# First row maxima of the second layer taken in the last expert steps of a two-layer transformer kernel

## The reference, cut to what matters

```
x = x + attention0(layernorm(x))     # causal, 16 heads of 8, with bias
x = x + experts0(layernorm(x))       # 8 experts, the best 2 of each row, 128 -> 512 -> 128, exact GELU
x = x + attention1(layernorm(x))     # no mask, 16 heads of 8
x = x + fp4_mlp(layernorm(x))        # gate, up, down (352 wide), each block of 16 rounded to FP4
```

## Time and profile before

| | |
|---|---|
| median of three runs | 2203.91 us |
| the profiled execution, its own time | 2203.53 us |
| its span in the profile | 2201.8 us |
| busy: TensorE, VectorE, ScalarE, GpSimd | 1959.7, 1631.8, 1428.1, 1127.5 us |
| expert stage, first and last expert matmul | 838.3 to 1109.6 us |
| layer_one, first matmul | 1113.27 us |

### The profile page before, as it was taken

How to read it: one execution, slowest core, us unless ns; L and a number is a source line. 1 busy time by engine, 2 the same in 40 slices (tenths; PEclk the granted TensorE clock), 3 DMA queues, 4 the chain that set the end, 5 groups by cost and what they waited for, 6 DMA issues and landing times. The chain is left out here.

```text
span 2201.8 us, 48376 instructions
## 1 busy us (share of the span) xinstructions
PE 1959.7 (89%) x13892; PEld 998.6 (45%) x14051; DVE 1631.8 (74%) x4372; ACT 1428.1 (65%) x3354; POOL 1127.5 (51%) x1882
## 2 busy tenths in 40 slices
PE   5999999999999957999969888899988889898985
PEld 1455555555555537999922223333333333333333
DVE  7888888887888734443367788888888887888855
ACT  0666766666676644555537777777777777777774
POOL 6334746546474263344345465656665665664221
PEclk7999999999999978999979999999999999999998
DMA  3342323222232122222322212122222212211100
GB/s 97 86 137 73 95 78 94 83 83 86 83 91 81 42 81 71 71 75 84 95 67 66 64 59 66 58 64 63 63 63 66 65 56 63 65 57 54 57 6 15
DMA packets 144100, 155.34 MB, mean 71 GB/s; under 512 B 32160, under 2 KB 111712, under 8 KB 143584
## 3 DMA queue, kind: packets, MB, share of 16 engines
q1 hardware_dynamic: 131888, 131.84, 20.0%
q0 software_dynamic: 8192, 16.79, 2.7%
q10 hardware_dynamic: 3760, 3.62, 0.6%
HBM read 102.87 MB, written 47.71 MB: 68 GB/s over the span
## 5 line engine op out<-in xcount | busy, mean ns | idle before, releaser
L2370 DVE TENSOR_REDUCE l_rowmax<-pair 128x2 f32<-128x1024 f32 x512 | 597.1, 1217 | 134.1 <-PE pair L2046 134.1
L2245 ACT ACTIVATE l_probs<-bank 128x512 f32<-128x512 f32 x1024 | 554.9, 602 | 86.1 <-PE bank L2057 60.7
L1008 DVE CUSTOM_DVE_ANT_0 pair<-pair,mask_rows_q 128x512 f32<-128x512 f32 (+3 forms) x1024 | 476.7, 519 | 80.0 <-PE pair L718 72.9
L887 ACT ACTIVATE l_probs<-bank 128x256 f32<-128x256 f32 (+3 forms) x769 | 307.9, 444 | 106.9 <-PE bank L732 102.7
L718 PE MATMUL pair<-k_stack,q_stack 96*128 96x512 bf16 (+3 forms) x1024 | 316.0, 313 | 22.0 <-DVE l_rowmax L1008 13.5
L2057 PE MATMUL bank<-q_stack,k_stack 128*128 128x512 bf16 x929 | 298.5, 387 | 28.8 <-ACT l_probs L2245 13.6
L2069 PE MATMUL bank<-l_probs,v_aug 128*32 128x512 f32 x2048 | 278.3, 615 | 4.4 <-ACT l_oT L2302 2.6
L2046 PE MATMUL pair<-k_stack,q_stack 64*128 64x512 bf16 x1024 | 178.3, 394 | 79.5 <-DVE l_rowmax L2370 70.1
L730 PE MATMUL bank<-q_stack,k_stack 128*128 128x384 bf16 (+3 forms) x720 | 212.9, 299 | 0.2
L744 PE MATMUL bank<-l_probs,v_aug 128*32 128x512 f32 (+3 forms) x2048 | 191.9, 447 | 20.5 <-ACT l_probs L887 18.1
L2057 PEld LDWEIGHTS bank<-q_stack,k_stack 128*128 128x128 bf16 x1024 | 74.9, 97 | 248.2 <-ACT l_probs L2245 138.1
(11 more groups left out here) (359 smaller groups left out, 3408.2 us busy)
## 6 DMA issues: line engine op xcount, KB each, us to landing
q_stack<-scratch SPq DMA_DIRECT2D x192, 96.0 KB
k_stack<-scratch SPq DMA_DIRECT2D x180, 96.0 KB
q_stack<-scratch SPq DMA_DIRECT2D x320, 48.0 KB
k_stack<-scratch SPq DMA_DIRECT2D x300, 48.0 KB
scratch<-l_q_parts SPq DMA_DIRECT2D x31, 384.0 KB, 2.5
scratch<-l_k_parts SPq DMA_DIRECT2D x30, 384.0 KB, 2.6
experts_rows<-rows_in SPq DMA_DIRECT2D x136, 64.0 KB, 1.8
rows_out<-experts_y SPq DMA_DIRECT2D x68, 128.0 KB, 1.8
```

Of the source, the lines that this page charges most:

```text
L887: nc.scalar.activation(probs[:, (a * HG + j) % PSLOTS, c0:S], bank[:, c0:S], ACT.Exp, scale=SCALE).then_inc(t_read, 1)
L1008: nc.vector.tensor_tensor_reduce(scores, scores, m["mask_rows_q"][:, S - keys(t):S], 1.0, LOWEST, ALU.add, ALU.max, rowmax[:, g % 2, c:c + ...
L2245: nc.scalar.activation(probs[:, (a * HG + j) % PSLOTS, :], bank[:, :], ACT.Exp, scale=SCALE).then_inc(t_read, 1)
L2370: nc.vector.tensor_reduce(largest, banks[:, :].rearrange("p (k n) -> p k n", k=2), X_AXIS, ALU.max).then_inc(s_read, 1)
```

## The change

It takes the maxima of the first eight quads (groups 0 and 1 of the first batch, steps 0 to 7 of layer_one) in the last eight expert steps, j = 60 to 67, and begins layer_one at step 8.

- TensorE: in step j, two of the four score matmuls before `hidden`, two after it, all into one PSUM pair (`bank_pairs[0]`), each waiting until VectorE has reduced the one before. That pair was where the rows were transposed; from step 61 on they are transposed into a free half of the output banks instead. In step 67 `turned_max` of group 0 follows, ahead of the last `expert_rows`.
- VectorE: two reductions a step after the copy of the transposed rows, before the bias add. `clear_queries` goes to GpSimd, behind its last weight copy, with `split_first_max` behind it.
- SyncE and ScalarE: two stack DMAs a step instead of one, so that all four groups are filled in the same 14 steps; `first_queries` and `first_keys` are gone. After step 67, SyncE waits for the turned maxima and issues the six DMAs of `stack_max`, then the last store.
- layer_one: `FIRST = 8`; projections of the second batch both at step 8; `third_gather` four at step 8, four at step 9.
- Three early pieces of the second batch (factors, normalise, transpose) move up by one expert step.

```diff
+EARLY_QUADS = 8
-    GATHER, ROWS, FACTORS, NORMALISE = (38, 46), (36, 51), (45, 60), (42, 57)
-    XNT, KEYS, QUERIES, VALUES = (43, 58), 45, 47, 49
+    GATHER, ROWS, FACTORS, NORMALISE = (38, 46), (36, 51), (45, 59), (42, 56)
+    XNT, KEYS, QUERIES, VALUES = (43, 57), 45, 47, 49
+    MAXIMA = expert_tiles(NB) // PAIR - EARLY_QUADS
...
             if 0 <= j - STACK[which] < STACK_DMAS:
-                g, n = divmod(j - STACK[which], STACK_DMAS // 2)
-                stack_part(eng, (q_stack, k_stack)[which], scratch, g, which, n, stacked[g])
+                for i in range(2):
+                    g, n = divmod(2 * (j - STACK[which]) + i, STACK_DMAS // 2)
+                    stack_part(eng, (q_stack, k_stack)[which], scratch, g, which, n, stacked[g])
...
                 if j + 3 < NJ:
                     load(j + 3)
+                if j == NJ:
+                    sp.wait_ge(max_copied, 1)
+                    stack_max(sp, q_stack, rowmaxT, 0, max_rows)
                 if j >= 1:
                     store(j - 1)
...
             for i in range(TT):
                 pool.wait_ge(gathered[i], 64)
+            for half in range(2):
+                clear_queries(half)
+                pool.wait_ge(queries_cleared, half + 1)
+            split_first_max()
...
+            def scores_for_max(j, pair):
+                g, t, n = max_of(j, pair)
+                if n == 0:
+                    pe.wait_ge(xT_ready, MAXIMA + 1)
+                else:
+                    pe.wait_ge(max_taken, n)
+                if n % (2 * TT) == 0:
+                    pe.wait_ge(stacked[g], 16 * STACK_DMAS)
+                for half in range(2):
+                    part, h_ = slice(HALF * half, HALF * (half + 1)), g * HG + pair + 2 * half
+                    last = nc.tensor.matmul(m["bank_pairs"][0][:, half * S:(half + 1) * S], q_stack[part, h_, t * P:(t + 1) * P],
+                                            k_stack[part, h_, :], start=True, stop=True)
+                last.then_inc(max_made, 1)
...
                 if j + 2 < NJ:
                     turned_rows(j + 2)
+                if j >= MAXIMA:
+                    scores_for_max(j, 0)
                 if 0 < j + 1 < NJ:
                     hidden(j + 1)
+                if j >= MAXIMA:
+                    scores_for_max(j, 1)
+                if j == NJ - 1:
+                    turned_max()
                 if j >= 0:
                     expert_rows(j)
...
+            act.wait_ge(max_turned, 1)
+            nc.scalar.copy(rowmaxT[:, :], y_bank[NJ % 2][:, BOTH:2 * BOTH].bitcast(BF16)[0:PARTS * HG * TT, 0:P]).then_inc(max_copied, 1)
...
-                    nc.vector.tensor_copy(rowsT[j % 2][:, :], xT_bank[j % 2][:, 0:BOTH]).then_inc(xT_ready, 1)
+                    nc.vector.tensor_copy(rowsT[j % 2][:, :], rows_bank(j + 2)).then_inc(xT_ready, 1)
+                if j >= MAXIMA:
+                    for pair in range(2):
+                        take_max(j, pair)
...
-                    if 0 <= j - (NJ - 3) < 2:
-                        clear_queries(j - (NJ - 3))
...
-    END = [("out", g, F + 4 * g + 6) for g in range(G)] + [("v", 0, 0), ("qk", 0, -9), ("qk", 1, -8)] + [
+    END = [("out", g, F + 4 * g + 6) for g in range(G)] + [("v", 0, 0), ("qk", 0, -9, set(range(2, NB))), ("qk", 0, -8, {1}), ("qk", 1, -8)] + [
...
-    ACT_WORK = [("first_keys", g, 3 * (g - 2)) for g in range(2, G)]
...
-    POOL_WORK += [("third_gather", k, -27 + (0, 1, 3, 4)[k // 2]) for k in range(2 * TT)]
+    POOL_WORK += [("third_gather", k, -24 + k // TT) for k in range(2 * TT)]
...
-    SP_WORK += [("first_queries", g, 3 * (g - 2)) for g in range(2, G)]
...
-    FIRST, LAST = 0, QUADS * (NB - 1) + F + 41
+    FIRST, LAST = EARLY_QUADS, QUADS * (NB - 1) + F + 41
```

More of the change, by code:

```diff
@@ L1324, in stack_early, with rows_bank, max_of @@
             if 0 <= j - STACK[which] < STACK_DMAS:
-                g, n = divmod(j - STACK[which], STACK_DMAS // 2)
-                stack_part(eng, (q_stack, k_stack)[which], scratch, g, which, n, stacked[g])
+                for i in range(2):
+                    g, n = divmod(2 * (j - STACK[which]) + i, STACK_DMAS // 2)
+                    stack_part(eng, (q_stack, k_stack)[which], scratch, g, which, n, stacked[g])
+        def rows_bank(j):
+            return xT_bank[j % 2][:, 0:BOTH] if j <= MAXIMA else y_bank[j % 2][:, BOTH:2 * BOTH]
+        def max_of(j, pair):
+            g, t = divmod(j - MAXIMA, TT)
+            return g, TT - 1 - t, 2 * (j - MAXIMA) + pair
         @block.sync
@@ L1423, in turned_rows, with turned_max @@
                     pe.wait_ge(xT_ready, j - 1)
+                if j > MAXIMA:
+                    pe.wait_ge(y_ready, j - 3)
                 for s in range(PAIR):
-                    last = nc.tensor.transpose(xT_bank[j % 2][:, s * P:(s + 1) * P], rows[j % LANES][:, s, :], ident[:, :])
+                    last = nc.tensor.transpose(rows_bank(j)[:, s * P:(s + 1) * P], rows[j % LANES][:, s, :], ident[:, :])
                 last.then_inc(xT_mm, 1)
+            def scores_for_max(j, pair):
[11 more added lines that the diff above has]
+                last.then_inc(max_made, 1)
+            def turned_max():
+                pe.wait_ge(rowmax_step, 4)
+                pe.wait_ge(y_ready, NJ - 1)
+                bank = y_bank[NJ % 2][:, BOTH:2 * BOTH].bitcast(BF16)
+                nc.tensor.transpose(bank[0:PARTS * HG * TT, 0:P], rowmax_parts[:, :, :].rearrange("p a n -> p (a n)"),
+                                    m["ident_bf"][:, :]).then_inc(max_turned, 1)
             def hidden(j):
@@ L1448, in expert_rows @@
                                         ident[0:rows_, 0:rows_])
+                if MAXIMA < j + 2 < NJ:
+                    pe.wait_ge(xT_ready, j + 3)
                 if early_turn(j) is not None:
@@ L1620, in take_early, with take_max @@
                     nc.vector.tensor_copy(v_aug[0][:, 2 * half:2 * half + 2, :, 0:D], bank.rearrange("p (t h d) -> p t h d", t=2, h=H))
-            def clear_queries(half):
-                rows = m["q_stack"][0][HALF * (1 - half):HALF * (2 - half), :, :].rearrange("p (g j) t -> p g (j t)", j=HG)
-                dve.wait_ge(w1_copied, PAIR * NJ)
-                nc.vector.memset(rows[:, :, 2 * half * S:2 * (half + 1) * S].bitcast(U32), 0).then_inc(queries_cleared, 1)
+            def take_max(j, pair):
+                g, t, n = max_of(j, pair)
+                dve.wait_ge(max_made, n + 1)
+                largest = rowmax[:, g % 2, :].rearrange("p (k i t) -> p i k t", k=2, t=TT)[:, pair, :, t]
+                nc.vector.tensor_reduce(largest, m["bank_pairs"][0][:, :].rearrange("p (k n) -> p k n", k=2), X_AXIS, ALU.max
+                                        ).then_inc(max_taken, 1)
             def upper_constants(i):
```

50 lines of the change are left out of this document (29 added, 21 removed).

## The result

The kernel before takes 2202.45 us (median of six runs, 2197.73 to 2206.95), the changed one 2210.97 us (six runs, 2208.63 to 2213.49). The ratio is 1.0033, with a 95% interval from 1.002 to 1.0047: slower by some 7 us (the two medians are 8.5 us apart). The time lies in the range that was given, but the forecast was no change that can be told, and this is one.

The account below looks back on a forecast made before the run. The prediction took TensorE, with SyncE as full, to bound the expert stage and GpSimd's chain layer_one's start. Expert stage +12.9 and start -10.1 gave +2.8 on 2203.5, so 2206.3 us, range 2198.5 to 2211.5.

Parts of the forecast that it names:

- Term 1: Expert steps 53 to 66: second stack DMA makes SyncE's step 4.80 us, so TensorE's step 65 starts 7.75 us late.
- Rival A: Expert stage: the second issue costs SyncE nothing, steps 60 to 64 are TensorE's; 2201.0 us, chance 0.12.
- rival C: Expert stage: SyncE pays the full 1.3 us for each second stack DMA; +8.8, 2212.3 us, chance 0.21.
- Term 2: Expert steps 60 to 64: maxima make TensorE's step 4.4 us, under SyncE's 4.80, so they cost nothing.
- Term 3: Expert steps 65 and 66: no rows to wait for, the maxima cost 0.6 us each, +1.2 us.
- Term 4: Step 66's end to layer_one's start: SyncE's six DMAs precede the last store, 9.4 us against 5.5, +3.9.
- Term 5: Expert stage: ScalarE's second stack DMA takes 0.53 us of its queue, within its waits for TensorE; costs nothing.
- Term 6: layer_one's start to the end of the statistics: GpSimd's chain takes 31.2 us, before 41.3; -10.1 us.
- Rival B: layer_one's start: GpSimd's chain does not bind, the whole 18.2 us are won; 2198.2 us, chance 0.15.
- forecast case: Whole kernel: +2.8 us to 2206.3 us, no change that can be told, own spread 2203 to 2209; chance 0.52.
- if that cover is gone: Expert steps 60 to 64 without SyncE's queue hiding the maxima: 5 x 0.6 = 3.0 us, less 0.5 of slack.

Follow-up runs that it names:

- after_again: The changed kernel itself run once more, on the chip of its variants: 2289.24 us, ratio 1.0033 to the kernel before.
- q_by_act: The changed kernel with every second DMA of the query stacks issued by ScalarE instead of SyncE: 2286.37 us, ratio 1.0008 to the kernel before.
- third_later: The changed kernel with layer_one's third-batch gathers at steps 10 to 13 and its combine, statistics and what follows four steps later: 2283.68 us, 0.9992 of the kernel before.
- max_by_act: The changed kernel with the six DMAs of the first group's maxima issued by ScalarE instead of SyncE: 2286.60 us, ratio 1.0009 to the kernel before.

## Why the prediction was right or wrong

- **Term 1, SyncE's queue: right.** 4.76 us a step on average for 4.80, and the last loads 8.5 us late (1105.22) for 8.25; alone it delays step 65 by 7.8 to 9.5 us for 7.75. Rival A (4.4 us apart) and C (over 5) are excluded by the same rows.
- **Term 2, the maxima of steps 60 to 64 "cost nothing, hidden by term 1": the step that failed.** It rested on TensorE's step being 3.8 + 0.6 = 4.4 us, under SyncE's 4.80. It is 5.39, so that TensorE and not SyncE set the pace. The 0.6 was the price of a quad in one piece (0.53) and a wait of 0.1. Measured, the four matmuls in two pieces cost 1.04, and the number loads that end up behind the wait 0.5 more. The prediction looked at what the waiting matmul's partner, VectorE, was doing, and found the wait itself rightly to be about nothing; it did not look at what else was queued behind that wait on TensorE's own queue. With 5.35 for 4.4 in its own sum, steps 60 to 65 would have given +7.8 rather than the +3.0 that it held hidden: the cover, 1.0 us a step, was smaller than what it should cover, 1.55.
- **Term 3, steps 65 and 66: mis-sized with the same number.** 1.2 was predicted; step 66's outputs end some 3.0 us late (1122.4 in the trace after), of which two steps at 1.55 more are the whole.
- **Term 4, the boundary: mechanism right, size 1.1 us off in this execution.** From step 66's end to layer_one 10.5 us for 9.4. All of the miss lies behind the last store's issue (3.70 for 2.35 us); up to there the chain ran as worked out, 6.7 for 7.0. In other executions of the same order the whole was 9.4 to 10.3 us. The half clock of the last outputs cost nothing, since the store stood behind the six DMAs in any case, as after_again shows at full clock (9.7 us from 1157.9 to 1167.60).
- **Term 5, ScalarE's second DMA and the early pieces: nothing, right as far as the rows show**; q_by_act even gives ScalarE a third.
- **Term 6, layer_one's start: right.** -10.9 for -10.1, the wait at the statistics 5.9 for 7 us. Rival B is out: the chain binds. But the prediction stopped there. third_later shows that most of the other 8 us could be had by moving the third batch, which the change had left at the head of GpSimd's work.
- **The chances.** Slower by over 0.2% had 0.25: 0.21 by rival C's mechanism, the rest a tail of the forecast case. The sign came true and that mechanism did not; no rival said that TensorE's own step could outgrow SyncE's, though the text priced that case ("if that cover is gone") at 3 us.
- **The range held by luck.** 2210.97 us is 0.5 us inside its upper end, which had been drawn for rival C; what brought the time there was term 2's cost, which no rival had. The forecast itself, no change that can be told, did not come true. And from layer_one's start on the time came back 1.9 us more than forecast (12.0 for 10.1); without that it would lie outside.

What stays open is why the clock fell in the last outputs of some executions and not of others, with the same matmuls and the same 1.51 us of idle time ahead of them: it fell in the changed kernel's first trace, q_by_act and third_later (3.44 to 3.67 us), and not in after_again and max_by_act (2.31 us). Open is also why the last store lands late in some.

## What to carry to other kernels

When work is put into a queue behind a new wait, list everything that follows the wait on that engine, its register reads too: in this loop they ran ahead beside other matmuls and cost nothing, and a wait that was itself free turned them into time. Price an inserted group of matmuls as it will stand, in how many pieces and between which others, not by its length where it stands alone. And a cover that hides a cost has to be compared with the whole new step, not with the old one plus the useful work; then ask what the emptied stretch will wait for next, and move that as well.

## What the runs showed that was not expected

- A pair of score matmuls placed alone between float32 matmuls takes 0.32 us of the engine and makes its neighbours 0.1 to 0.2 us longer; the quad in one piece takes 0.53 us. Two pieces a step cost 1.04 us.
- The read of a register behind a waiting matmul costs 0.5 us a step for two reads of 0.30 us, and nothing from the second step on when it stands ahead; the first step with early reads loses 0.6 to 1.0 us.
- The same six DMAs took SyncE 4.05 to 4.10 us in four executions and 4.56 in another, ScalarE 4.57.
- A third issue a step on ScalarE did not lengthen TensorE's waits for its GELUs (0.9 us in all, 1.5 before the edit).
- After 1.51 us without work the granted clock was 0.57 in the next 4 us of one execution (outputs 3.44 us), while the same outputs took 2.31 us in another; it fell in three of five such executions.
